# First attention's front, its outputs by eight steps, and expert sums in two arrays, in a two-layer decoder kernel

## The reference

```python
xc = conv over the sequence, 3 taps per channel         # (1, 2048, 256)
xs = xc + xc @ pe_w.T
q, k, v = split(xs @ qkv_w.T), 16 heads of 16, bfloat16
attn = softmax(q @ k.T / 4); o = attn @ v               # as coded: x is (1, 2048, 256)
```

```python
_, idx = jax.lax.top_k(logits.T, top_k)                 # 128 rows for each expert
h = gelu(xn[idx] @ fc1.T + b1); y = h @ fc2.T + b2      # hidden size 1024
output   = zeros.at[flat_idx].add(y * gate)             # a row can be picked by several
gate_sums = zeros.at[flat_idx].add(gate)
output = where(gate_sums > 0, output / gate_sums, output)
```

## Time and profile before

| | us |
|---|---|
| median of 3 runs (lowest, highest) | 3483.79 (3481.06, 3496.04) |
| the profiled execution | 3490.16 |
| its span in the trace | 3488.4 |
| PE, DVE, POOL, ACT busy | 3141.9, 2374.8, 1732.6, 1705.4 |
| front of the first attention (0 to 86.57) | 86.57 |
| attention loop (86.57 to 720.00) | 633.43 |
| experts, first to last bias addition (2178.3 to 2306.0) | 127.7 |

### The profile page before, as it was taken

How to read it: one execution, slowest core, us unless ns; L and a number is a source line. 1 busy time by engine, 2 the same in 40 slices (tenths; PEclk the granted TensorE clock), 3 DMA queues, 4 the chain that set the end, 5 groups by cost and what they waited for, 6 DMA issues and landing times. The chain is left out here.

```text
span 3488.4 us, 63848 instructions
## 1 busy us (share of the span) xinstructions
PE 3141.9 (90%) x24201; PEld 1812.1 (52%) x24201; DVE 2374.8 (68%) x5271; ACT 1705.4 (49%) x2086; POOL 1732.6 (50%) x1163
## 2 busy tenths in 40 slices
PE   6899999989999999999999972868989999999797
PEld 3666666654555555555555531756655434444346
DVE  5999999955566565655665647136528978888518
ACT  1788888842444444444444441223233666666641
POOL 2888888823777777777777840223461000000012
PEclk9999999989999999999999985989997999999898
DMA  1200000010000000000000033830011111111101
GB/s 46 53 2 2 2 2 2 2 40 16 4 1 4 1 4 1 3 4 1 4 1 1 1 108 115 269 76 1 1 34 26 18 18 18 18 21 15 33 1 37
DMA packets 61305, 87.31 MB, mean 25 GB/s; under 512 B 9457, under 2 KB 51314, under 8 KB 60146
## 3 DMA queue, kind: packets, MB, share of 16 engines
q1 hardware_dynamic: 57970, 79.22, 9.0%
q0 software_dynamic: 3072, 4.34, 0.7%
HBM read 60.24 MB, written 8.54 MB: 20 GB/s over the span
## 5 line engine op out<-in xcount | busy, mean ns | idle before, releaser
L922 DVE TENSOR_REDUCE x0hm<-x0pM 128x1 f32<-128x400 f32 (+1 forms) x1024 | 520.3, 562 | 379.3 <-PE x0pM L824 379.3
L403 POOL TENSOR_SCALAR rows<-rows,mb 128x1024 bf16<-128x1024 bf16 x512 | 567.3, 1119 | 129.2 <-DVE mb L355 129.2
L349 DVE TENSOR_SCALAR_CACHE_REDUCE rows<-pS 128x1024 bf16<-128x1024 f32 x512 | 616.8, 1206 | 1.1 <-PE pS L298 1.1
L414 ACT ACTIVATE prT<-pP 128x1024 bf16<-128x1024 bf16 x512 | 523.4, 1024 | 116.5 <-PE pP L309 116.1
L1386 DVE TENSOR_REDUCE x1hm<-x1pM 128x1 f32<-128x400 f32 (+1 forms) x1024 | 518.7, 566 | 66.1 <-PE x1pM L1272 62.9
L1505 ACT ACTIVATE x1pr<-x1pST 128x1024 f32<-128x1024 f32 (+1 forms) x416 | 403.9, 1022 | 216.5 <-PE x1pST L1324 216.4
L784 POOL TENSOR_TENSOR x0acc<-x0acc,x0pr 128x1024 f32<-128x1024 f32 (+1 forms) x176 | 421.5, 2395 | 110.6 <-ACT x0pr L1033 94.8
L784 POOL TENSOR_TENSOR x0acc<-x0acc,o_nat 128x1024 f32<-128x1024 f32 (+1 forms) x176 | 419.4, 2383 | 71.9 <-ACT o_nat L1033 53.1
L1033 ACT ACTIVATE o_nat<-x0pST 128x1024 f32<-128x1024 f32 (+1 forms) x208 | 213.0, 1024 | 279.6 <-PE x0pST L868 279.3
L1033 ACT ACTIVATE x0pr<-x0pST 128x1024 f32<-128x1024 f32 (+1 forms) x208 | 212.9, 1024 | 279.4 <-PE x0pST L868 279.1
L2605 POOL MEMSET f_tri<- 128x128 f32 x1 | 0.2, 209 | 674.6 <-POOLq L1177 674.6
(11 more groups left out here) (364 smaller groups left out, 5157.8 us busy)
## 6 DMA issues: line engine op xcount, KB each, us to landing
m_w<-in_moe_w1T SPq DMA_DIRECT2D x16, 1024.0 KB, 10.0
m_w<-in_moe_w2T SPq DMA_DIRECT2D x16, 1024.0 KB, 7.0
x1sq<-x1qh SPq DMA_DIRECT2D x32, 128.0 KB, 4.0
x1sk<-x1kh SPq DMA_DIRECT2D x32, 100.1 KB, 3.6
rows_d<-m_xr SPq DMA_DIRECT2D x1, 2176.0 KB, 7.8
acc_d<-m_zero SPq DMA_DIRECT2D x4, 514.0 KB, 7.4
m_acc<-acc_d SPq DMA_DIRECT2D x4, 514.0 KB, 8.0
g_xN<-in_x SPq DMA_DIRECT2D x1, 2048.0 KB, 9.1
```

The source lines that it names most:

```text
L349: nc.vector.tensor_scalar(rows[u][:, half * 1024:(half + 1) * 1024], pS[half][:, :], 1.0, None, ALU.mult, ALU.max, accum_out=mx[u][:, half ...
L403: nc.gpsimd.tensor_scalar(r, r, -1.0, mb[u][:, 0:1], ALU.mult, ALU.add).then_inc(s_df, 1)
L414: nc.scalar.activation(prT[u][:, half * 8:(half + 1) * 8, :], pP[half][:, :, :], ACT.Exp, scale=-1.0 / HD ** 0.5).then_inc(s_ex, 1)
L922: emptied(nc.vector.tensor_reduce(hm[g % 2][:, a, t, i % 8 // 2:i % 8 // 2 + 1], bank(name)[:, 0:w], AX.X, ALU.max, negate=True), name)
```

## The change

- **Front**: tap 0 of the convolution is an ACT activation with a scale. xs is written into `G.xN` (the buffer in which x is kept later) and lives on into the loop with `wqkv`. Only value tile 0 is made here. SP issues the q rows, each as soon as its own part of `qT` is cleared; ACT issues the k rows, after its copies of the first two q units.
- **Value tiles 1 to 15** are made inside the loop, `value_tile`, one per head at its step 11, into the second half of a `pO` bank; ACT copies each after step 13 of the head (`value_rows`). The load of x into `G.xN` waits for the last.
- **Outputs** are taken for eight steps at a time, in steps 5 and 13 of 16, from two banks of eight. DVE's hardware loop has 16 steps instead of 4, ACT's too (with the copy); POOL's is as it was.
- **Experts**: even experts scatter into one array, odd ones into another, each with its own semaphore. The gather for e + 4 stands ahead of the scatter's wait. The block no longer waits for the last scatter.
- **Self attention of layer 1**: SP waits for both arrays' scatters, loads both for every chunk, DVE adds the two gate sums and adds both arrays' sums to x.
- **Semaphores** are set back by POOL at the start of two later blocks, not between parts with a barrier.

```diff
+        def rows_of(queue, x, cs, cols, sem, zeroed=None):
             for c in cs:
                 mine = slice(16 * (c % 8), 16 * (c % 8) + 16)
                 if x == "q":
+                    if zeroed is not None:
+                        queue.wait_ge(zeroed, c + 1)
                     for a in range(2):
                         queue.dma_start(qT[64 * a:64 * a + HD, c, cols], qp[mine, c // 8, cols]).then_inc(sem, 16)
...
-                    sp.wait_ge(s_zero, 24)
                     sp.wait_ge(s_q, 2)
-                    rows_of(sp, "q", range(16), first, s_first)
-                    sp.wait_ge(s_k, 2)
-                    rows_of(sp, "k", range(16), first, s_first)
+                    rows_of(sp, "q", range(16), first, s_first, s_zero)
...
-                        for j in range(DJ):
-                            nc.vector.tensor_scalar(xc[:, j, cols], xp[:, j, n * 512:n * 512 + 512], cw[:, j, 0:1],
-                                                    None, ALU.mult).then_inc(s_tap, 1)
                         for i in (1, 2):
                             for j in range(DJ):
-                                dve.wait_ge(s_tap, 4 * n + 2 * (i - 1) + j + 1)
+                                if i == 1:
+                                    dve.wait_ge(s_tap0, 2 * n + j + 1)
+                                else:
+                                    dve.wait_ge(s_tap, 2 * n + j + 1)
                                 ins = nc.vector.scalar_tensor_tensor(
...
+                    act.wait_ge(s_edge, 2)
+                    act.wait_ge(s_cw, 16)
+                    act.wait_ge(s_in, 16)
+                    first_tap(0)
+                    act.wait_ge(s_in2, 16)
+                    for n in range(1, 4):
+                        first_tap(n)
+                    queries(0)
+                    act.wait_ge(s_k, 2)
+                    act.wait_ge(s_zero, 24)
+                    rows_of(act, "k", range(16), first, s_firstk)
+                    for n in range(1, 4):
+                        queries(n)
+                    act.wait_ge(s_full, place["v", 0, 0] + 1)
+                    nc.scalar.activation(v1[:, 0, :, 0:HD],
+                                         bank(("v", 0, 0))[:, 0:D].rearrange("p (c d) -> p c d", d=HD),
+                                         ACT.Copy).then_inc(s_va, 1)
...
+            pOV = [m2.ps(f"pO{i}", [P, 512]) for i in range(2)]
+            pO = [b[:, 0:8 * (HD + 1)].rearrange("p (a d) -> p a d", a=8) for b in pOV]
+            pV = pOV[0][:, 256:256 + D]
...
+                    sp.wait_ge(s_vt, NT - 1)
                     sp.dma_start(G.xN[:, :, :], A["x"].rearrange("(t p) d -> p t d", p=P)).then_inc(G.s_x, 16)
...
+                    def value_tile(t):
+                        for k in range(DJ):
+                            mm = nc.tensor.matmul(pV, xs[:, k, t * P:(t + 1) * P], wqkv[:, k, 2 * D:3 * D],
+                                                  start=(k == 0), stop=(k == 1))
+                        mm.then_inc(s_vt, 1)
+
                     def values(n, u, part):
                         if part == 0:
                             pe_.wait_ge(s_ex, 2 * n + 2)
-                            if u % 2 == 0 and n >= 4:
-                                pe_.wait_ge(s_oc, n - 2)
+                            if n % 8 == 0 and n >= 16:
+                                pe_.wait_ge(s_oc, n - 8)
+                            if n % 16 == 0 and n >= 16:
+                                pe_.wait_ge(s_va, n // 16 + 1)
+                            if n % 16 == 11 and n // 16 + 1 < NT:
+                                pe_.wait_ge(s_oc, n - 3)
+                                value_tile(n // 16 + 1)
                         for kt in range(8 * part, 8 * part + 8):
-                            mm = nc.tensor.matmul(pO[u // 2][:, u % 2, :], prT[u][:, kt, :], v1[:, n // 16, kt, :],
...
-                        outputs = u % 2 == 1 and (not isinstance(n, int) or n >= 7)
-                        b = (u - 7) % NU // 2
+                        outputs = k % 8 == 5 and (not isinstance(n, int) or n >= 13)
+                        b = (k - 13) % 16 // 8
                         if outputs:
-                            sums(n - 7, b)
...
                         if outputs:
-                            quotients(n - 7, b)
-
-                    run(dve, step)
+                            quotients(n - 13, b)
+
+                    for n in range(16):
+                        step(n, n)
+                    with dve.Fori(1, NS // 16) as h:
+                        for k in range(16):
+                            step(h * 16 + k, k)
                     maximum(NS - 1, NU - 1)
-                    for n in (NS - 6, NS - 4, NS - 2):
-                        for part in (sums, recip, quotients):
-                            part(n, n % NU // 2)
+                    for part in (sums, recip, quotients):
+                        part(NS - 8, 1)
...
+                    def value_rows(h):
+                        act.wait_ge(s_vt, h + 1)
+                        nc.scalar.activation(v1[:, bass.ds(h + 1, 1), :, 0:HD],
+                                             pV.rearrange("p (o c d) -> p o c d", o=1, d=HD), ACT.Copy).then_inc(s_va, 1)
+
+                    def head(h):
+                        for k in range(16):
+                            step(h * 16 + k, k % NU)
+                            if k == 13:
+                                value_rows(h)
+
+                    head(0)
+                    with act.Fori(1, NT - 1) as h:
+                        head(h)
+                    for n in range(NS - 16, NS):
+                        step(n, n % NU)
...
+                nc.clear_and_free_semaphores(G.used_up)
...
+                    if c >= 2:
+                        sp.wait_ge(s_r3, 8 * (c - 1))
+                    for i in range(2):
+                        sp.dma_start(ex[i][:, 4 * (c % 2):4 * (c % 2) + 4, :], acc_d[i][c * QG:(c + 1) * QG, :]
+                                     .rearrange("(t p) n -> p t n", p=P)).then_inc(s_ex3[c], 16)
+
+                for i in range(2):
+                    sp.wait_ge(G.s_sc[i], 16 * 8)
...
+                    here = slice(4 * (c % 2), 4 * (c % 2) + 4)
+                    dve.wait_ge(s_ex3[c], 32)
+                    nc.vector.tensor_tensor(ct[:, g], ex[0][:, here, D], ex[1][:, here, D], ALU.add).then_inc(s_d3, 1)
+                    dve.wait_ge(s_d3, 4 * c + 1)
+                    nc.vector.tensor_scalar(fl[:, g], ct[:, g], 0.0, None, ALU.is_le).then_inc(s_d3, 1)
+                    dve.wait_ge(s_d3, 4 * c + 2)
+                    nc.vector.tensor_tensor(dn[:, g], fl[:, g], ct[:, g], ALU.add).then_inc(s_d3, 1)
+                    dve.wait_ge(s_d3, 4 * c + 3)
                     nc.vector.reciprocal(rd[:, g], dn[:, g]).then_inc(s_d3, 1)
...
+                    dve.wait_ge(s_d3, 4 * c + 4)
+                    for i in range(2):
+                        for t in range(4 * c, 4 * c + 4):
+                            if i == 1:
+                                dve.wait_ge(s_r3, 8 * c + t % 4 + 1)
+                            nc.vector.scalar_tensor_tensor(G.xN[:, t, :], ex[i][:, t % 8, 0:D], rd[:, t:t + 1],
+                                                           G.xN[:, t, :], ALU.mult, ALU.add).then_inc(s_r3, 1)
                     for t in range(4 * c, 4 * c + 4):
-                        nc.vector.scalar_tensor_tensor(G.xN[:, t, :], ex[:, t, 0:D], rd[:, t:t + 1], G.xN[:, t, :],
-                                                       ALU.mult, ALU.add).then_inc(s_r3, 1)
-                        dve.wait_ge(s_r3, t + 1)
+                        dve.wait_ge(s_r3, 8 * c + 4 + t % 4 + 1)
...
-                    for q in range(4):
-                        sp.dma_start(acc_d[512 * q:512 * q + 512, :].rearrange("(t p) n -> p t n", p=P),
-                                     zero[:, :, :]).then_inc(s_out, 16)
+                    for i in range(2):
+                        for q in range(4):
+                            sp.dma_start(acc_d[i][512 * q:512 * q + 512, :].rearrange("(t p) n -> p t n", p=P),
+                                         zero[:, :, :]).then_inc(s_out, 16)
...
-                        if e:
-                            pool.wait_ge(s_sc, 16 * e)
-                        nc.gpsimd.indirect_dma_start(
-                            acc_d, bass.IndirectOffsetOnAxis(ic[e][:, 0:1], 0), ct[e % 2][:, :], None,
-                            compute_op=ALU.add).then_inc(s_sc, 16)
                         if e + ROWS < E:
                             gather(e + ROWS)
-                    pool.wait_ge(s_sc, 16 * E)
+                        if e >= 2:
+                            pool.wait_ge(s_sc[e % 2], 16 * (e // 2))
+                        nc.gpsimd.indirect_dma_start(
+                            acc_d[e % 2], bass.IndirectOffsetOnAxis(ic[e][:, 0:1], 0), ct[e % 2][:, :], None,
```

(10 more changed lines are left out.)

87 lines of the change are left out of this document (38 added, 49 removed).

## The result

| | before | after |
|---|---|---|
| median, us (lowest, highest; 5 runs each) | 3483.79 (3477.76, 3496.04) | 3460.81 (3456.37, 3465.61) |
| profiled execution, span | 3488.4 | 3459.0 |

The changed kernel is faster by 23 us: a ratio of 0.9927, with a 95% interval of 0.9903 to 0.9952. Forecast were 3439 and a range of 3418 to 3472. So the sign and the range held, and the gain is half of the forecast one. That is luck.

A forecast was written before the change was run, and what follows sets the result against it. VectorE was taken to bound the attention loop, with nothing full but the DMA engines (0.77) among the experts. Terms −27.1 − 3.5 − 18.0 + 3.5 = −45.1 gave 3445 profiled, 3439 us on the median, range 3418 to 3472.

The forecast's parts named there:

- Front, −27.1: Before the loop: first tap on ACT starts TensorE 14.0 us sooner; moving 15 value tiles into the loop saves 13.1.
- Rival D: Front: ACT's and SP's issues share something, 48 at 1.3 us each, TensorE stalls, +9 us: 3448; chance 0.09.
- Loop, −3.5: Attention loop: outputs taken per eight steps save 5.0 us, value tiles cost 1.5; bounds −20 and +5.
- The floor: Attention loop: maximum mb ends no sooner than GpSimd's running pair, so a step takes at least 2.42 us.
- Rival C: Attention loop: GpSimd's pair does not hold mb and all of −20 us arrives: 3423; chance 0.08.
- B: Attention loop: the longer VectorE body fetches code at 14 back edges, 1.3 us each, +18: 3457; chance 0.20.
- E: Attention loop: two code reads in sequence at each back edge, 4.8 us uncovered, 67 us: 3506, slower; chance 0.05.
- Experts, −18.0: Experts: gather ahead of the scatter's wait removes TensorE's 22.6 us of waits, less 4.6 for DMA; bounds −22.6 and −10.9.
- what it took to be late next: Experts: DMA at share 0.77 needs 7.7 us per expert against 7.0; up to 6.3 come back, 4.6 taken.
- The bound of 9 waits of 1.3: Experts: a gather's flight of 7.4 us against 6.1 leaves at most 1.3 for each of 9 waits, 11.7.
- Hand-over and chunks, +3.5: Fourth attention part: TensorE begins 0.8 us sooner, the second array's additions cost later chunks 4.3; bounds −1 and +7.
- The rest, 0: Untouched code from the self attention's last statistics to the end: forecast to change by 0 us.

The follow-up runs named there:

- e5: Kernel before, with GpSimd's clears of qT and kT held back until VectorE's first two taps; first pair of taps 0.88 us, front gained 14.4 us.
- e9: Kernel before, with a memset and a 128x8 tensor_scalar at VectorE's start; that tensor_scalar took 22.50 us, TensorE started at 27.00.
- e12: Kernel before, with one wait ahead of the fourth of GpSimd's clears; two taps took 2.18 us, TensorE started at 12.22, first rounding 16 us earlier.
- e1: Changed kernel, with the loop's maximum mb as a one-input tensor_reduce instead of a tensor_tensor; loop 614.1 us instead of 626.9.
- e3: Changed kernel, with six buffers for gathered rows instead of four; the 16 contributions took 104.7 us instead of 115.8.
- e4: Changed kernel, with one array of sums again, gather still ahead of the scatter's wait; experts 115.3 us, span 3441.4, 17.6 under the changed kernel's.

## Why the prediction was half right

**Front, −27.1: right in size and cause.** −27.2. e5 shows that the clears held the tap. The prediction set a lock for the length of one instruction beside the 18.10 and wrote that the trace agrees. A clear takes 0.95, so a lock of that length does not give 18; it was the whole row, as e9 and e12 show. The step to ACT did not depend on it. Rival D did not come: 48 issues on two queues ran beside each other at 0.64 each on ACT.

**Loop, −3.5: right.** −4.7, and 19.62 us for eight steps where 19.60 was worked out. The floor was read from one row of 0.32 before; e1 shows it directly. Value tiles cost nothing that shows, where 1.5 us were charged; that is the 1.2 by which the forecast was short. That every other step of the old loop was already held at the floor was read wrongly: mb lasts its plain 0.15 there, and VectorE's own work makes the 2.42 (two roundings of 1.14, mb and the sums 0.07 each). Rival C (no floor) is wrong, and e1 shows what it would be worth: 12.8 us more.

**Rivals B and E: wrong.** The median of 3460.8 lies near B's 3457, but not through B: no VectorE wait stands at a back edge, and the instruction queue carried 70 packets instead of 68 (69 in the other kernels with this loop). A reader who had only the time would have taken B for the cause.

**Experts, −18.0: the size failed, −11.9.** The step that failed is what it took to be late next. It let a flight of 7.4 against 6.1 cost nothing in the middle estimate and charged 4.6 to the DMA's share instead. The gathers' flight, from issue to use, stayed at 7.3 us or more, and its waits and what hangs on them cost 11.1; the DMA's share cost nothing (e3, with TensorE busy for all of the 100 us at the same 0.81). The bound of 9 waits of 1.3, which leaves a gain of 10.9, came close, but in part by luck. Two of its 9 waits lay ahead of the stretch, so the waits to be won were 16.6 and not 22.6. And 4.9 of the gain came from TensorE's clock, which no longer fell; the prediction had a clock of 0.95 in its rows and gave it no term. The second array was rightly free of waits for scatters, and e4 shows that it wasn't needed for that.

**Hand-over and chunks, +3.5: the price of the second array was too low, and the pair of profiles overstates it.** The two terms of the forecast, −0.8 and +4.3, stand against −0.6 and +10.1. Of these +9.5, 5.7 lie ahead of the fourth chunk's additions, and 4.7 of the 5.7 between those of the third chunk and those of the fourth (27.6 us instead of 22.9). The term that was mis-sized is VectorE's additions at 0.46 each. In the third chunk three of them ran beside GpSimd's rows and took 0.84 to 1.58, the eight together took 5.44, and TensorE waited 6.4 us behind them instead of 3.4. Single additions of these two chunks had taken 0.82 and 1.18 in the kernel before, too; the 0.46 was read from the first two chunks. It is the same lock between two-input instructions and GpSimd's reads by which the loop's floor was argued, and it was not applied here. The other 3.8 lie behind the fourth chunk's first addition (203.4 us instead of 199.6), where kernels with the old code took 199.4 to 203.0: they are not shown to be the change's. TensorE's mean granted clock over the stage was 0.93 in the profile of before and 0.91 in that of after; e5, with the old code and 0.91, took 288.4 us, against 294.1.

**The rest, 0: +4.3.** 2.2 are a step with one fall of TensorE's clock; the other 2.1 were not traced. All fourteen runs vary by 10 us there.

**From the profiled execution to the median.** The profile of before was 6.4 us above its median, and that of after equal to its own (3459.0 and 1.8 make 3460.8). The two profiles differ by 29.4, the medians by 23.0. In a later session the kernel before had a median of 3492.81 over 11 runs, 9 above the first one, so neither difference is good to better than some us. The forecast carried 6.4 over in full, which is right only if the excess of one execution lies in stages that a change leaves alone.

## What to carry to other kernels

Where a wait in a queue of DMAs is moved, ask first which transfer's flight is then the longest against the work that covers it, and give it more buffers; that was worth 11.1 us here, about as much as the change had gained among the experts (11.9). Before work is split over two arrays to free a wait, add up what joining them costs, and on an engine that shares its time with GpSimd count each two-input instruction at the length of the GpSimd instruction it may meet. Where a row of GpSimd clears runs at the start of a kernel and VectorE has a tensor_scalar to do, try one wait in the row; here it brought the first rounding 16 us forward.
